# Three graph aggregations in a four-layer GNN kernel: products with the low parts of the edge counts are replaced by products with one or two copied source tiles

## The chip, the cores and the metric

The kernel runs on one core of a Trainium2 chip. The metric is the time of one execution on the device in microseconds (us), the median of several runs. Engines are named as in the profile: PE is TensorE, DVE VectorE, ACT ScalarE, POOL GpSimd, and SP the queue of the sync engine, which issues most DMAs.

## The reference

512 nodes with 512 features, 8192 edges (`src`, `dst`), four residual layers with a normalisation ahead of each. The first is a sparse attention with a feed-forward part. The second is a mean aggregation: the sum of the sources' features over a node's edges, divided by their number, through `W_l`, plus the node's own features through `W_r`, then a normalisation over the nodes. The third is two graph convolutions with self loops and degree scaling, the fourth a sum aggregation with a two-layer perceptron. What the change concerns:

```python
h = jnp.maximum(_layernorm(x), 0.0)
agg = jax.ops.segment_sum(h[src], dst, num_segments=512)      # layer 2, then divided by the degree
out = jax.ops.segment_sum(h[src] * norm[:, None], dst, n)     # layer 3, twice, with self loops
```

## The kernel before, in words

The edges are turned on the chip into a matrix of counts: how many edges go from each source node to each node. `c1` holds it by source tiles. An aggregation is then a matmul of the node features with `c1`. All matrices with 512 rows are held as four tiles of 128 rows (NT = 4).

Matmuls run in a rounded 32-bit format (`fp32r`). To keep precision, each operand is split into a high part (rounded) and a low part (the rest), and a product is made of three: high by high, high by low, low by high. For `c1` the high part is `c1_hi` (in the buffer of `q_t`) and the low part `c1_lo` (in that of `k_t`); VectorE makes them at L1009 and L1010 while the feed-forward part runs. A product of two 512 x 512 matrices has 4 x 4 matmuls of [128 x 128] by [128 x 512] per kind, so 48 in all.

TensorE runs its instructions in the order written, and waits on semaphores where it must. In the order of time:

- Attention (L1494 to L1504): 16 units `n` of two heads each. Per unit TensorE turns exponentials (`e_turn`, L1461), makes scores two units ahead (L1447) and weights values (L1476). ScalarE makes the exponentials (L507), VectorE the minima (`lowest`, L905), the weights (`weigh`, L917), every second unit a normalisation (L925 to L927), and a few side jobs tied to a unit: sums of degrees (L958, in units 5, 7, 9, 11) and an added bias (L968, in units 6, 8, 10, 12). Around the first unit ScalarE takes the four tiles of transposed counts out of PSUM (`counts_out`, L494).
- First aggregation (L1534 to L1550): for each source tile k, wait for the high part of `h1` (ScalarE, L374, `z_sb_rounded`), then 4 matmuls with the high and 4 with the low part of the counts; then 16 transposes of `h` (L1197); then 16 matmuls with the low part of `h1` (L1547; VectorE makes it at L625 in `v_sb`), the last four of which release the mean (L1030). The linear layer follows (L1562 on).
- Second aggregation (L1595, `product_by_row`, its lines L1228 and L1233): as the first, with `y` (high part by ScalarE at L512 in `v_sb`, low part by VectorE at L625 in `z_sb`). The low products go bank by bank; VectorE scales each bank (L1117) for the next layer.
- Third aggregation (L1601, `product_in_parts`, its lines L1251, L1270 and L1271): the counts are on the left; bank by bank 4 products high by high, then 4 pairs of high by low and low by high. The high part of the features comes from ScalarE (L512), the low part from VectorE (L636). Behind each bank VectorE adds, takes moments and makes layer norm coefficients (L1152 on), ScalarE makes the high part for the fourth layer (L374, `t_sb_rounded`), and that layer's aggregation with other counts (L1604) begins.

SP issues DMAs and waits in the order of its program: the blocks of the attention's edge weights (L287, from `z_sb` to `big`, ended by a wait at L292), a copy of the counts (L300), the weights (`load`, L312: `w1_0`, `w2_0`, `w_lr`, `w1_2`, `w2_2`, `w_3`, each after a matmul stage that frees its room in `big`), the four stores (L328). The load of `w1_2` (2 MB) is issued when the feed-forward part's last matmul is done, just as the first aggregation begins. The last four of the 36 rows of `big` hold no weights.

## Time and profile before

| what | us |
|---|---|
| runs: median (lowest to highest) | 397.31 (396.34 to 402.98) |
| profiled execution: span from the first to the last instruction | 395.7 |
| profiled execution: TensorE busy | 371.7 |
| profiled execution: VectorE busy, ScalarE busy | 313.2, 171.5 |

The mean granted clock of TensorE in the profiled execution is 0.992 of full speed. The profile tells of one execution by its span; what lies around the span is in the times of the runs only, whose median is 1.6 above it. Instructions of an engine can overlap, so a matmul's duration is not its share of the time. A line of the chain of waits says what the end of the kernel depended on, in order of time.

### The profile page before, as it was taken

Reading aid. Unit: us, or ns where it says so; the run is one execution under the profiler, and the core shown is the slowest. Engines: PE = TensorE matmul, PEld = TensorE weight load, DVE = VectorE, ACT = ScalarE, POOL = GpSimd, SP = SyncE. Lnnn points to the kernel's source line nnn. Section 1 sums busy time; section 2 is a strip of 40 time slices with the busy share of each in tenths; the row PEclk is TensorE's granted clock in tenths of the full one; section 3 lists DMA queues with packets and bytes.
Section 4 is the critical chain, followed back from the end, with each engine's and each line's share of the span. In section 5 each row is a group of like instructions: output and inputs, shape, how many; then the busy total and the mean of one; then the engine's idle time right before and its main releaser. Section 6 shows DMA issues by size and latency. Waiting matters only on the chain.

```text
span 395.7 us, 5097 instructions
## 1 busy us (share of the span) xinstructions
PE 371.7 (94%) x1781; PEld 282.1 (71%) x1781; DVE 313.2 (79%) x660; ACT 171.5 (43%) x287; POOL 4.2 (1%) x19
## 2 busy tenths in 40 slices
PE   2889999999988999999989999999799999999994
PEld 1555666666757888887768788887578878787873
DVE  5889999999947779997886978499875778488346
ACT  5664666444136224343467723361363531135320
POOL 4000000000000000000000000000000000000000
PEclk9999999999998999999999999999999999999998
DMA  7602444343226000056500230400420032000002
GB/s 240 247 1 69 157 154 135 104 133 110 73 85 208 2 2 1 2 188 243 206 2 1 100 114 14 198 2 0 134 81 0 2 116 96 2 0 0 2 2 104
DMA packets 16360, 32.92 MB, mean 83 GB/s; under 512 B 1360, under 2 KB 1488, under 8 KB 16336
## 3 DMA queue, kind: packets, MB, share of 16 engines
q1 hardware_dynamic: 15744, 32.25, 23.6%
q10 hardware_dynamic: 592, 0.36, 0.3%
q8 instruction: 15, 0.25, 0.3%
q14 instruction: 9, 0.07, 0.1%
HBM read 21.07 MB, written 1.05 MB: 56 GB/s over the span
## 4 chain that ended last, share of the span: by engine, by line
PE 78%; DVE 14%; ACT 4%; issue 3%; DMA 1%; DVEq 0%; ACTq 0%
PE acc L1391 11%; PE bank L1373 10%; PE bank L1476 7%; PE bank L1270 6%; PE bank L1271 6%; PE bank L1251 4%; PE acc L1251 4%; PE acc L1271 4%; PE acc L1270 4%; PE bank L1461 4%; PE acc L1447 3%; DVE big_rounded L652 2%; PE acc L1228 2%; PE bank L1228 2%; PE acc L1540 2%
## 5 line engine op out<-in xcount | busy, mean ns | idle before, releaser
L1391 PE MATMUL acc<-wide_rounded,c_rounded 128*126 128x512 f32 x200 | 58.2, 435 | 0.7 <-ACT acc L464 0.7
L1391 PEld LDWEIGHTS acc<-wide_rounded,c_rounded 128*126 128x126 f32 x200 | 37.2, 187 | 17.8 <-issue 10.7
L792 DVE TENSOR_SCALAR wide_rounded<-iota_f,picked 128x512 fp32r<-128x512 f32 x100 | 42.6, 482 | 2.1 <-issue 1.1
L483 ACT COPY z_sb<-acc 126x512 f32<-126x512 f32 x37 | 21.6, 585 | 44.9 <-PE acc L1391 36.2
L507 ACT ACTIVATE wide<-wide,low_col 128x512 f32<-128x512 f32 x32 | 21.3, 715 | 32.8 <-DVE low_col L905 32.8
L1476 PEld LDWEIGHTS bank<-v_sb,big 128*128 128x128 f32 x256 | 29.7, 192 | 4.7 <-issue 4.3
L625 DVE TENSOR_TENSOR wslot_rounded<-wslot,wide_rounded 128x512 fp32r<-128x512 f32 x24 | 16.2, 688 | 21.3 <-ACT wslot L377 21.3
L1476 PE MATMUL bank<-v_sb,big 128*128 128x65 f32 x256 | 31.6, 277 | 0.0
L798 DVE TENSOR_TENSOR c_rounded<-row_bc,wslot_rounded 128x1008 fp32r<-128x1008 bf16 x25 | 30.0, 1201 | 0.0
L1373 PE MATMUL bank<-t_sb,wslot 128*128 128x512 f32 x64 | 29.5, 594 | 0.5 <-ACT t_sb L459 0.5
L652 DVE TENSOR_TENSOR big_rounded<-big,big_rounded 128x1024 fp32r<-128x1024 f32 x24 | 29.1, 1222 | 0.4
L369 ACT ACTIVATE std<-mv,eps_c 128x1 f32<-128x1 f32 x20 | 5.8, 290 | 39.4 <-DVE mv L657 25.9
L905 DVE CUSTOM_DVE_ANT_0 wide<-acc,t_sb 128x512 f32<-128x512 f32 x32 | 20.7, 684 | 1.7 <-PE acc L1447 1.6
L917 DVE TENSOR_TENSOR big<-bank,big 128x512 f32<-128x512 f32 x32 | 20.6, 684 | 1.4 <-PE bank L1461 1.4
L1461 PE MATMUL bank<-ident,wide 128*128 128x128 f32 x128 | 18.3, 285 | 2.7 <-ACT wide L507 2.7
L1373 PEld LDWEIGHTS bank<-t_sb,wslot 128*128 128x128 f32 x64 | 12.0, 189 | 11.5 <-issue 9.6
L488 ACT COPY acc<-zero_c 126x512 f32<-126x512 f32 x33 | 19.4, 588 | 1.0
L1271 PE MATMUL acc<-big_rounded,wslot_rounded 128*128 128x512 f32 x48 | 18.7, 389 | 0.0
L1270 PE MATMUL acc<-big_rounded,wide_rounded 128*128 128x512 f32 x48 | 18.7, 389 | 0.0
L1461 PEld LDWEIGHTS bank<-ident,wide 128*128 128x128 f32 x128 | 15.0, 151 | 4.2 <-ACT wide L507 3.6
L374 ACT ACTIVATE wide_rounded<-bank,col 128x512 fp32r<-128x512 f32 x12 | 8.3, 694 | 17.4 <-PE bank L1271 17.4
L1373 PE MATMUL bank<-wslot,t_sb 128*128 128x512 f32 x32 | 15.0, 592 | 0.0
(314 smaller groups left out, 768.8 us busy)
## 6 DMA issues: line engine op xcount, KB each, us to landing
big<-z_sb SPq DMA_DIRECT2D x36, 252.0 KB
big<-in_w SPq DMA_DIRECT2D x4, 2048.0 KB, 7.8
x_sb<-in_x SPq DMA_DIRECT2D x8, 256.0 KB, 4.7
big<-in_w_3t SPq DMA_DIRECT2D x2, 1024.0 KB, 6.8
row_bc<-in_rows SPq DMA_DIRECT2D x7, 256.0 KB, 6.6
wslot<-in_wq SPq DMA_DIRECT2D x1, 1024.0 KB, 8.9
wslot<-in_wk SPq DMA_DIRECT2D x1, 1024.0 KB, 10.8
wslot<-in_wv SPq DMA_DIRECT2D x1, 1024.0 KB, 12.8
```

Source lines behind the costliest of these rows:

```text
L483: nc.scalar.copy(stage[0:BROWS, b % STAGES, :], a).then_inc(S["staged"], 1)
L507: nc.scalar.activation(e, e, ACT.Exp, bias=low_col[:, n // 4, h:h + 1], scale=-1.0).then_inc(S["e_ready"], 1)
L652: nc.vector.tensor_tensor(lo.rounded[:, part, :], lo.full[:, part, :], hi.rounded[:, part, :].bitcast(F32), ALU.subtract).then_inc(S[name ...
L792: nc.vector.tensor_scalar(hot_ring[:, u, k, :], iota_f[:, :], picked[:, 0, s0 + k:s0 + k + 1], None, ALU.is_equal)
L798: nc.vector.tensor_tensor(st_ring[:, u, :, :, :], mask[:, c, :, :].rearrange("p s a w -> p (s a) w").unsqueeze(3).broadcast_to([P, 2 * GRO ...
L1251: nc.tensor.matmul(bank[banks[m]][:, :], tile(a[0], m), r[0], start=(k == 0 and not started), stop=False)
L1270: nc.tensor.matmul(bank[b][:, :], tile(a[0], m), r[1], start=False, stop=False)
L1271: last = nc.tensor.matmul(bank[b][:, :], tile(a[1], m), r[0], start=False, stop=(k == len(terms) - 1))
L1373: ins = nc.tensor.matmul(to[:, :], left, right, start=(k == 0), stop=(k == NT - 1))
L1391: last = nc.tensor.matmul(to, st_ring[:, u, 2 * k + a, :, :].rearrange("p w k -> p (w k)"), hot_ring[:, u, k, :], start=False, stop=False, ...
L1461: last = nc.tensor.transpose(tile(bank[4 + a], t), tile(held_e[:, i % HELD, :], t), ident[:, :])
L1476: last = nc.tensor.matmul(o, by_head[:, t, h, m * P:(m + 1) * P], v_sb[:, t, h, :], start=(t == 0), stop=(t == NT - 1))
```

## The change

[...] With 8192 edges, only one source node can have more than 4096 edges to one node; with a self loop added, two can. The changed kernel multiplies with the counts' low parts of only one source tile in the first aggregation and of two in the second and third. Which tiles these are is found on the chip. ScalarE's four `counts_out` also sum the counts of each source node (`out_deg`). VectorE makes a key of each (degree times 1024 plus the node's place) in unit 3. SP copies the 512 keys into one row. VectorE takes the eight largest in unit 10, turns the first two into tile numbers and makes the second differ from the first. SP reads both numbers into registers and copies the tiles that they name (256 KB each) to fixed places, the last four rows of `big`, so that TensorE's program stays as it was built: `star_c` for the counts' low part, `star_hi` for the features' high part. TensorE waits for the copies ahead of the first product with them (`starred`, m = 0). Lines that only declare buffers and semaphores are left out below.

```diff
         bn_t = wide[:, NT:, :]
+        key_row = iota_f[0:1, :]
+        star_hi = both(lambda a: a[:, NT * KW - 4:NT * KW - 2, :], big, big_r)
+        star_c = both(lambda a: a[:, NT * KW - 2:NT * KW, :], big, big_r)
         b2_rows = [k_t_r[0:1, 0, :], k_t_r[0:1, 1, :]]
...
                              ).then_inc(S["rows_in"], 16)
+            sp.wait_ge(S["keys_ready"], 1)
+            sp.dma_start(key_row.rearrange("a (p t) -> a p t", t=NT), row_key[:, :]).then_inc(S["keys_row"], 16)
             sp.wait_ge(S["st_mm"], UNITS)
...
             load("w2_0", w2_0)
+            sp.wait_ge(S["tops_ready"], 1)
+            tops_at = [sp.value_load(top_tiles[0:1, j:j + 1], min_val=0, max_val=NT - 1) for j in range(2)]
+            def star(to, j, source, done):
+                sp.dma_start(to.rounded[:, j:j + 1, :].bitcast(F32),
+                             source.rounded[:, bass.ds(tops_at[j], 1), :].bitcast(F32)).then_inc(S[done], 16)
+            def all_hi(name):
+                hi_by, before_hi, _, _ = parts[name]
+                sp.wait_ge(S[hi_by], before_hi + NT)
             sp.wait_ge(S["ff1_mm"], FT)
...
             load("w1_2", w1_2)
+            sp.wait_ge(S["c1_parts_ready"], NT)
+            star(star_c, 0, c1_lo, "c_star_in")
+            all_hi("h1")
+            star(star_hi, 0, z_at, "h1_star_in")
             sp.wait_ge(S["lin1_mm"], NT)
             load("w2_2", w2_2)
+            sp.wait_ge(S["loops_added"], NT)
+            for j in range(2):
+                star(star_c, j, c1_lo, "loops_star_in")
+            all_hi("y")
+            for j in range(2):
+                star(star_hi, j, spare_at, "y_star_in")
             sp.wait_ge(S["gcn1_mm"], FT)
             load("w_3", w1_3t, 0)
             load("w_3", w2_3t, 1)
+            all_hi("gcn_out")
+            for j in range(2):
+                star(star_hi, j, spare_at, "gcn_star_in")
             for t in range(NT):
...
                            allow_small_or_imprecise_dtypes=True).then_inc(S["tables"], 1)
+            nc.gpsimd.iota(row_key[:, :], [[P, NT]], base=0, channel_multiplier=1,
+                           allow_small_or_imprecise_dtypes=True).then_inc(S["key_base"], 1)
             nc.gpsimd.memset(pick, 0.0).then_inc(S["pick_zeros"], 1)
...
                 act.wait_ge(S["c2_turned"], t + 1)
-                nc.scalar.copy(c1[:, t, :], bank[4 + t][:, :]).then_inc(S["c1_ready"], 1)
+                nc.scalar.activation(c1[:, t, :], bank[4 + t][:, :], ACT.Copy, accum_out=out_deg[:, t:t + 1]
+                                     ).then_inc(S["c1_ready"], 1)
             counts_out(1)
...
                     on_diagonal(rcnt_bc, rcnt_c)
+                if n == 3:
+                    dve.wait_ge(S["c1_ready"], NT)
+                    dve.wait_ge(S["key_base"], 1)
+                    nc.vector.scalar_tensor_tensor(out=row_key[:, :], in0=out_deg[:, :], scalar=float(KEYS),
+                                                   in1=row_key[:, :], op0=ALU.mult, op1=ALU.add
+                                                   ).then_inc(S["keys_ready"], 1)
+                if n == 10:
+                    dve.wait_ge(S["keys_row"], 16)
+                    link(nc.vector.max(top_keys[:, :], key_row))
+                    link(nc.vector.tensor_copy(top_i[:, :], top_keys[:, 0:2]))
+                    link(nc.vector.tensor_scalar(top_tiles[:, :], top_i[:, :], P.bit_length() - 1, NT - 1,
+                                                 ALU.logical_shift_right, ALU.bitwise_and))
+                    link(nc.vector.tensor_tensor(same_tile[:, :], top_tiles[:, 0:1], top_tiles[:, 1:2],
+                                                 ALU.is_equal))
+                    nc.vector.tensor_tensor(top_tiles[:, 1:2], top_tiles[:, 1:2], same_tile[:, :],
+                                            ALU.bitwise_xor).then_inc(S["tops_ready"], 1)
                 if n == 4:
...
                 return [((S[hi_by], before_hi + k + 1), (S[lo_by], before_lo + k + 1)) for k in range(n)]
-            def product_by_row(banks, lhs, rhs, ready, done):
+            def starred(to, m, left, right, n, done):
+                for ready in done if m == 0 else ():
+                    pe.wait_ge(S[ready], 16 * n)
+                for j in range(n):
+                    last = nc.tensor.matmul(to, tile(left.rounded[:, j, :], m), right.rounded[:, j, :], start=False,
+                                            stop=(j == n - 1))
+                return last
+            def product_by_row(banks, lhs, rhs, ready, done, star=None):
                 terms = list(zip(lhs, rhs))
                 for n, (a, r) in enumerate(terms):
                     pe.wait_ge(*ready[n][0])
-                    for i in range(2):
+                    for i in range(1 if star else 2):
                         for m, b in enumerate(banks):
...
                         last = nc.tensor.matmul(bank[b][:, :], tile(a[1], m), r[0], start=False,
-                                                stop=(n == len(terms) - 1))
+                                                stop=(not star and n == len(terms) - 1))
+                    if star:
+                        last = starred(bank[b][:, :], m, star_hi, star_c, 2, star)
                     last.then_inc(S[done], 1)
             def product_in_parts(banks, lhs, rhs, ready, done, group=1, weight_lo=None, second=None, started=False,
-                                 by_tile=0, free={}):
+                                 by_tile=0, free={}, star=None):
...
                         nc.tensor.matmul(bank[b][:, :], tile(a[0], m), r[1], start=False, stop=False)
-                        last = nc.tensor.matmul(bank[b][:, :], tile(a[1], m), r[0], start=False,
-                                                stop=(k == len(terms) - 1))
+                        if not star:
+                            last = nc.tensor.matmul(bank[b][:, :], tile(a[1], m), r[0], start=False,
+                                                    stop=(k == len(terms) - 1))
+                    if star:
+                        last = starred(bank[b][:, :], m, star_c, star_hi, 2, star)
                     last.then_inc(S[done], 1)
...
                 pe.wait_ge(*reads("h1")[k][0])
-                for i in range(2):
-                    for m in range(NT):
-                        nc.tensor.matmul(bank[m][:, :], tile(h1[k][0], m), c1s[k][i], start=(k == 0 and i == 0),
-                                         stop=False)
+                for m in range(NT):
+                    nc.tensor.matmul(bank[m][:, :], tile(h1[k][0], m), c1s[k][0], start=(k == 0), stop=False)
             pe.wait_ge(S["h_ready"], 2 * NT)
...
                 for m in range(NT):
-                    last = nc.tensor.matmul(bank[m][:, :], tile(h1[k][1], m), c1s[k][0], start=False,
-                                            stop=(k == NT - 1))
-                    if k == NT - 1:
-                        last.then_inc(S["agg1_mm"], 1)
+                    nc.tensor.matmul(bank[m][:, :], tile(h1[k][1], m), c1s[k][0], start=False, stop=False)
+            for m in range(NT):
+                starred(bank[m][:, :], m, star_hi, star_c, 1, ("c_star_in", "h1_star_in")).then_inc(S["agg1_mm"], 1)
             lo_w, hi_w = weights["w_lr"]
...
             pe.wait_ge(S["loops_added"], NT)
-            product_by_row(hi, halves(spare_at, z_at), halves(c1_hi, c1_lo), reads("y"), "agg2_mm")
+            product_by_row(hi, halves(spare_at, z_at), halves(c1_hi, c1_lo), reads("y"), "agg2_mm",
+                           star=("loops_star_in", "y_star_in"))
             product_in_parts(lo + hi, weight("w1_2", NT), halves(t_at, t_lo), reads("gcn_in"), "gcn1_mm",
...
                              weight_lo="w2_2_lo")
-            product_in_parts(hi, halves(c1_hi, c1_lo), halves(spare_at, z_at), reads("gcn_out"), "agg2b_mm")
+            product_in_parts(hi, halves(c1_hi, c1_lo), halves(spare_at, z_at), reads("gcn_out"), "agg2b_mm",
+                             star=("gcn_star_in",))
             pe.wait_ge(S["c2_ready"], NT)
```

## Rows read from the trace of the kernel before

**Rows 1.** The page: busy time of each engine, its share, instructions.

```profile
PE 371.7 (94%) x1781; PEld 282.1 (71%) x1781; DVE 313.2 (79%) x660; ACT 171.5 (43%) x287; POOL 4.2 (1%) x19
```

**Rows 2.** The chain of waits in order of time: start us, us, what.

```profile
118.03 0.59 ACT c L494
...
245.41 7.26 PE acc L1540 x32
...
288.11 7.53 PE bank L1228 x32
...
295.64 3.63 PE bank L1233 x16
...
346.62 0.91 PE bank L1251 x4
...
354.78 7.59 PE acc L1228 x32
```

**Rows 3.** The timeline of the first aggregation: start us, us, engine, line, operation.

```profile
245.44 0.37 SPq L312 DMA_DIRECT2D big<-in_w  x1
...
247.84 0.81 ACT L374 ACTIVATE z_sb_rounded<-x_sb,shift,rstd 128x512 fp32r<-128x512 f32 x1 [0.42 <-DVE shift L666]
...
252.51 1.91 PE L1197 MATMUL bank<-ident,h_sb 128*128 128x128 f32 x16
...
254.17 3.89 PE L1547 MATMUL acc<-q_t_rounded,v_sb_rounded 128*128 128x512 f32 x16
...
257.90 1.10 PE L1562 MATMUL bank<-t_sb_rounded,big_rounded 128*128 128x512 f32 x4
```

**Rows 4.** Half-microsecond window: busy us of five engines, PEclk, DMA share, GB/s.

```profile
252.00:252.50 0.50, 0.50 (x3) 0.34 (x3) 0.00 (x0) 0.00 (x0) 0.00 (x0) 1.00 0.26 98
```

**Rows 5.** The DMA issues: operands, count, KB each, median us from issue to landing.

```profile
out_x<-z_sb SPq DMA_DIRECT2D x4, 256.0 KB, 2.0
```

**Rows 6.** The timeline of SP's queue: the last copy of an attention block.

```profile
112.23 0.80 SPq L287 DMA_DIRECT2D big<-z_sb  x1
```

**Rows 7.** The waits of SP's queue: us in total, times, longest us.

```profile
SPq L292 <- DMA big<-z_sb: 2.2, 1, 2.2
```

**Rows 8.** The waits of all engines (columns as in rows 7).

```profile
PEld acc L1391 <- issue: 10.7, 41, 1.1
```

**Rows 9.** The timeline of the second aggregation.

```profile
292.01 0.82 ACT L512 ACTIVATE v_sb_rounded<-x_sb,shift,rstd 128x512 fp32r<-128x512 f32 x1
...
293.63 1.40 DVE L625 TENSOR_TENSOR z_sb_rounded<-z_sb,v_sb_rounded 128x512 fp32r<-128x512 f32 x2 [0.45 <-ACT z_sb L567]
```

**Rows 10.** The timeline of the third aggregation and the layer norm behind it.

```profile
343.54 0.69 ACT L512 ACTIVATE v_sb_rounded<-acc,dinv_c 128x512 fp32r<-128x512 f32 x1 [4.76 <-PE acc L1271]
...
344.26 0.75 DVE L636 SCALAR_TENSOR_TENSOR z_sb_rounded<-acc,dinv_c,v_sb_rounded 128x512 fp32r<-128x512 f32 x1 [4.50 <-ACT v_sb_rounded L512]
...
349.38 0.75 DVE L1152 SCALAR_TENSOR_TENSOR h_sb<-bank,dinv_c,row_bc 128x512 f32<-128x512 f32 x1 [0.30 <-PE bank L1271]
...
359.13 0.80 ACT L374 ACTIVATE t_sb_rounded<-x_sb,shift,rstd 128x512 fp32r<-128x512 f32 x1
```

**Rows 11.** One line's instructions (L422, an activation that also sums): ns min/median/max.

```profile
L422 ACT ACTIVATION_READ_ACCUMULATOR h_sb<-x_sb x2: 186/186/187, 5.7 to 6.3; 128x1 f32 x2
```

**Rows 12.** The groups by shape on VectorE: count, busy us, mean ns, idle.

```profile
L958 DVE TENSOR_REDUCE deg<-big 128x1 f32<-128x512 f32 x4 | 2.7, 676 | 0.0
...
L858 DVE TENSOR_SCALAR rounds_i<-pairs_i 1x1 int32<-1x1 int32 x1 | 0.1, 142 | 0.0
```

**Rows 13.** The timelines of ScalarE and TensorE in the attention, unit twelve.

```profile
163.88 1.33 ACT L507 ACTIVATE wide<-wide,low_col 128x512 f32<-128x512 f32 x2 [3.13 <-DVE low_col L905]
...
165.30 1.13 PE L1461 MATMUL bank<-ident,wide 128*128 128x128 f32 x8
```

**Rows 14.** Windows around two idle stretches of TensorE (columns as in rows 4).

```profile
119.50:122.50 3.00, 3.00 (x15) 3.00 (x15) 2.27 (x5) 0.75 (x2) 0.00 (x0) 0.50 1.01 290
...
282.50:284.50 2.00, 0.00 (x0) 0.00 (x0) 1.79 (x9) 0.85 (x2) 0.00 (x0) 1.00 0.78 224
```

More of the change, by code:

```diff
@@ L44 @@
 FLOOR = -3e38
+KEYS = 1024
+EXACT = 4096
+assert E < 2 * EXACT + 1 and N <= KEYS and E * KEYS + N < 2 ** 24
 ENDS, PICK, NEEDS = 130, 200, 400
@@ L134, in gnn_kernel @@
         bn_mean = sb("bn_mean", [P, NT])
+        out_deg = sb("out_deg", [P, NT])
+        row_key = sb("row_key", [P, NT])
+        top_keys = sb("top_keys", [1, 8])
+        top_i = sb("top_i", [1, 2], I32)
+        top_tiles = sb("top_tiles", [1, 2], I32)
+        same_tile = sb("same_tile", [1, 1], I32)
         rsum = sb("rsum", [P, NT, 4])
@@ L239, in gnn_kernel @@
             "agg2_mm", "agg2_ready", "gcn1_mm", "gcn1_ready", "gcn2_mm", "gcn2_ready", "agg2b_mm", "agg3_mm",
-            "agg3_ready", "gin1_mm", "gin1_ready", "gin2_mm", "b2_rows", "out_ready")}
+            "agg3_ready", "key_base", "out_degs", "keys_ready", "keys_row", "tops_ready", "c_star_in", "h1_star_in", "y_star_in",
+            "loops_star_in", "gcn_star_in", "gin1_mm", "gin1_ready", "gin2_mm", "b2_rows", "out_ready")}
         parts, made = {}, {"hi_scalar": 0, "lo_vector": 0}
```

## The prediction

> **What bounds the kernel now.** I read the busy times first: TensorE has work for 94% of the span [rows 1], so matmuls taken away should count. But its busy time is an average, so I next read the chain of waits in order of time, around the three places where the change takes matmuls away [rows 2]. The reader is to see that TensorE issues without a break in the first aggregation (32 matmuls from 245.41 in 7.26 us: 0.227 us each) and in the second (32 from 288.11, then 16 in 3.63 from 295.64). One matmul is under way for longer, but they overlap (four of them end 1.10 after the first began [rows 3]); what one gives back is the pace, and that only if the next one's operand is there. So I read the timelines of the three places for the time at which the last operand arrives, and the copies' rows for when a new one would.
>
> **The matmuls.** Each aggregation multiplies high by high, high by low and low by high parts, 16 matmuls each. The change takes out the 16 with the counts' low parts (k_t) and puts in 4, 8 and 8 with the copied tiles: 28 fewer, 6.4 us at 0.227. Their number is fixed when the program is built, whatever the counts are. All times below are on the clock of the profiled execution (span 395.7 us; the runs' median is 397.31, so 1.6 lies around the span).
>
> **First aggregation: -2.0.** TensorE now issues its first matmul at 245.24 (the chain counts it from 245.41 [rows 2]) and goes on to the linear layer at 257.90 [rows 3]. With high by high alone, the first three tiles need 12 x 0.227 = 2.7 and end at 247.96. The fourth tile's high part is written until 247.84 + 0.81 = 248.65 [rows 3], so 0.74 of the gain is a wait. From 248.70: 4 matmuls (0.91), the 16 transposes (254.17 - 252.51 = 1.66), the 16 with the low parts (257.90 - 254.17 = 3.73), 4 with the copy (0.91): 255.9 in place of 257.9, if the copy is there at 255.0. The copy of h1's tile waits for the high parts (248.7) and queues on SP behind the load of w1_2 issued at 245.44 [rows 3] and the copy of the counts' tile. The load is through by about 252.1 (in the window at 252.0 the share has fallen to 0.26) [rows 4]. Two copies of 256 KB, an eighth of the load each, are at most 2 x 6.7 / 8 = 1.7 more: 253.8, and I put 0.6 for the way to the semaphore, out of the 2.2 that a copy took in all [rows 7]: 254.4. Hidden, with 0.6 to spare; from 255.0 on each us is paid, and at 257.0 the gain is gone. VectorE's work behind (the rest of h1's transpose, weights, the mean) starts from the transposes, 2.9 earlier, so it doesn't take the 2.0 back. Bounds: -2.0 and 0.
>
> **Price of a pair of copies.** No copy from SBUF to SBUF of one [128, 512] tile stands in the trace. A store of 256 KB lands 2.0 after its issue [rows 5]; the last copy of an attention block (252 KB, SBUF to SBUF) took SP 0.80 to issue [rows 6] and 2.2 more to land [rows 7], 3.0. Both copies of a pair share a semaphore, so the second one counts: one issue later, 0.37 [rows 3] to 0.80. The source's address comes from a register, which no DMA here has; the nearest are TensorE's matmuls with such an address, which waited for their issue 41 times for 10.7 in all, 0.26 each, at most 1.1 [rows 8]. Low end 0.4 + 2.0 = 2.4, with no address work; high end 0.8 + 3.0 + 1.1 + 0.3 = 5.2; I take 2 x 0.25 + 0.4 + 2.2 = 3.1, near the store, which has the tile's form.
>
> **Second aggregation: +1.3.** The last high part of y is written until 292.83 and its low part until 295.03 [rows 9]. Before, the 16 matmuls with the counts' low parts filled the time up to 295.64. After, TensorE idles in short pieces until the fourth low part, then the wait for both copies holds it: 292.9 + 3.1 = 296.0. Two matmuls end the first bank at 296.4, and three banks of 6 (4.1) follow: 300.5 in place of 299.3. What is queued behind that wait on TensorE is all of the other banks' low products, which need no copy. Even with a copy at no cost the end is 295.1 + 21 x 0.227 = 299.9, so +0.6; at 5.2 it is +3.3. VectorE's first scaling starts at about the same time as before.
>
> **Third aggregation: +0.6.** The last high part is written until 344.23 and the low part until 345.01 [rows 10]. The pair lands at 344.3 + 3.1 = 347.4; the first bank ends at 347.8 in place of 346.6 [rows 2], d = 1.2 late, with TensorE idle for 2.0 before. The later banks take 10 matmuls, not 12 (2.3 for 2.7), but VectorE's chain of add, statistics and coefficients takes nearly 2.7 a tile itself: it idles 0.30 before the second [rows 10] and not before the others. So the last tile's high part for the next aggregation comes at 359.93 [rows 10] + d - 0.3, and TensorE, which before went through its 32 matmuls from 354.78 in 7.59 [rows 2], is through with them d - 0.6 later: +0.6. With a free copy d is -0.9 and the gain 1.5; at 5.2 it is +2.7.
>
> **Finding the tiles: +1.3.** Four copies of the counts out of PSUM also sum: a read of the accumulator of 0.186 [rows 11] and some 0.03. Two lie ahead of the first exponential, on the chain (118.03) [rows 2], one ahead of the third: +0.6; the other waits for transposes anyway. The key of 128x4 on VectorE and its copy into one row come seven units before they are needed: 0. The search is one maximum over 512 elements, priced as the reduction of 512 (0.68), and four links of 0.14 and some 0.04 between [rows 12]: 1.4. It stands ahead of unit 12's scores. Their exponentials, two from 163.88 in 1.33, end at 165.21; the first is ready at 164.55 and TensorE takes it at 165.30, the second at 165.8 [rows 13]. So 0.65 is covered: 1.4 - 0.7 = +0.7. Bounds: 0 (maximum at half that) to +1.8 (links of 0.4). SP reads the two indices after the loads of w1_0 and w2_0, while it only waits: 0. VectorE's wait for the row of keys stands ahead of all its attention work, but the row is sent seven units (some 26 us) earlier: 0, and each us that it were late would be paid in full. On SP the copies and their waits stand between the loads of w1_2, w2_2, w_3 and the stores; each waits for something that comes before the next load's own trigger, so no load moves: 0, up to the 0.6 that a copy takes of the transfer time of a load beside it.
>
> **Sum.** -2.0 + 1.3 + 0.6 + 1.3 = +1.2: 396.9 for the span, 398.5 by the runs. A measurement of this kernel tells about 2% (7.9 us) from no change; this is within it.
>
> **Rivals.** (A) The copies are cheaper than waits can see: 2.4 or less and addresses at no cost. Then -2.0, +0.6, -1.5, and +0.6 for the sums alone: -2.3, 395.0. For it: the store's 2.0 [rows 5]. Against: two issues in a row, and 3.0 for the nearest copy between SBUF tiles [rows 6, 7].
> (B) The copies sit at the high end, and the first one comes too late behind w1_2: 0 + 3.3 + 2.7 + 2.4 = +8.4, 405.7; halfway, 402. For it: SP's issue of up to 0.8 and unknown address work. Against: every copy finds an empty queue but the first.
> (C) Slower, by the clock. TensorE's granted clock is 0.50, the lower level of 1.2 GHz, through 119.5 to 122.5, behind the pause in which ScalarE empties the counts (118.03) [rows 2, 14]; yet through 282.5 to 284.5 TensorE did nothing and the clock stayed at 1.00, 2.4 GHz [rows 14]. The change makes a pause of 2.0 in the third aggregation and broken work of some 3.3 idle in 8 in the second. If either lets the clock fall for as long as at 119.5 (over 3 us busy at half pace), each costs about 1.7: 400.2 or 401.9. It passes 2% (7.9 - 1.2 = 6.7 lost) only if the low clock lasts 13.4 us of matmuls, for instance into the second graph convolution's first layer: then some 406. For: a pause of less than 2 sufficed once. Against: a longer one didn't, behind dense 512-column matmuls as here.
> The Trainium skill, in TensorE: Matmul & The Clock Gate, section "HAM oscillation — how this bites in real kernels", says that bursts of matmuls parted by waits for a DMA can find the clock gated at the start of each burst. By that rule both aggregations with a waited-for pair would start slow, and the time would be 401.9; by the row at 282.5 neither would, and it would be 398.5. The trace bears out both once, so the rule keeps a chance of its own, below the forecast's.
>
> **Chances.** Forecast (397 to 400) 0.55; A 0.16; B 0.14, a third of it past 2%; C 0.13, a quarter of it past 2%; 0.02 for a gain that I don't see. Eight in ten: from A's 395.0, a little below for the noise of the runs, to B's halfway point: 394.5 to 402.5. Slower by over 2%: 0.05 + 0.03 = 0.08, faster by over 2%: 0.02, within: 0.90.
>
> **What would show it.** Right: 1781 matmuls become 1753; the three aggregations' 48 matmuls 36, 40 and 40; from the first to the linear layer 10.7 us, not 12.7; in the second and third TensorE waits for a DMA ahead of the first copied product, some 0.7 and 2.0; from the copied y's last high part to its landing 3.1; in unit 12 TensorE waits 0.7 for ScalarE. Wrong: no such wait (A), waits of 3 and more (B), a granted clock under 1.00 behind 296 or 347 (C), or SP late for the first copy, so that the linear layer waits.

## The result, and the profile after

The changed kernel takes 400.46 us (median of 20 runs, 398.05 to 404.4), the kernel before, beside it, 398.52 (20 runs, 396.34 to 403.14): a ratio of 1.0056, 95% interval 1.003 to 1.0082. By the ratio that is 2.2 us more, between 1.2 and 3.3. The ratio leaves out each kernel's slowest runs, so it is not quite that of the two medians, which are 1.9 apart. I had forecast +1.2 us and no change by a measurement of 2%.

The matmuls went as the program says:

```profile
PE 373.4 (93%) x1753; PEld 279.8 (70%) x1753; DVE 314.4 (78%) x666; ACT 172.1 (43%) x291; POOL 4.2 (1%) x20
```

28 fewer than in [rows 1], and yet TensorE is busy for 373.4 us and not 371.7. (That the low parts left out are zero is the program's own premise: it takes counts of up to 4096 for exact, `EXACT` in the kernel. The runs give times and say nothing on it.) The reason for the longer busy time is the granted clock: the profiled execution (403.44 us, span 401.7) is one of the long ones, and TensorE stood at 0.50, the lower level of 1.2 GHz, in four pieces of some 3.4 us; e1 below, with the same 1753 matmuls and two such pieces, is busy for 368.2. In a window (busy us of TensorE, PEclk, DMA share, GB/s) one of them looks so:

```profile
350.00:352.00 2.00, 2.00 (x6) 0.50 0.00 0
```

In the profile of before there is one such piece under work (119 to 123 us, [rows 14]) and one behind the last matmul. A busy share, and a whole span, therefore can't be compared between two single executions here. What can be is the length of a stretch between two events, where the clock stood at full speed in both. I cut the kernel at first matmuls and read the same six stretches from the timelines of every kernel. A star marks a stretch in which the clock fell while TensorE still had work.

| from ... to (us) | before | after | e1 | e2 | e3 | e4 | e5 | e6 | e7 | e8 | e9 |
|---|---|---|---|---|---|---|---|---|---|---|---|
| first scores ... first turned exponentials | 4.82 | 6.45* | 4.99 | 4.82 | 4.99 | 5.00 | 4.81 | 7.10* | 6.47* | 4.99 | 5.00 |
| unit 11 ... unit 12 of the attention | 3.70 | 4.94 | 3.70 | 3.71 | 4.94 | 4.94 | 3.70 | 3.70 | 4.94 | 4.94 | 4.94 |
| first aggregation ... first keep-warm matmul | 40.02 | 38.05 | 37.88 | 38.05 | 38.34* | 37.90 | 38.08 | 38.01 | 37.92 | 38.00 | 38.34* |
| keep-warm ... first matmul behind the second aggregation | 13.85 | 15.48 | 15.47* | 15.43 | 14.57* | 15.47* | 13.82 | 13.85 | 15.04* | 15.47 | 15.20* |
| from there ... first matmul behind the product with the second counts | 66.82 | 69.01* | 67.47 | 67.46 | 66.83 | 65.66 | 66.80 | 65.69 | 67.53 | 67.50 | 67.54 |
| from there ... end | 29.77 | 31.16* | 31.08* | 31.17* | 29.45 | 31.14* | 29.53 | 31.13* | 31.07* | 31.21* | 29.55 |

**First aggregation.** The timeline of after (start us, us, engine, line, operation; in brackets the idle time ahead and what ended it), against [rows 3]:

```profile
248.00 2.89 PE L1613 MATMUL acc<-q_t_rounded,z_sb_rounded 128*128 128x512 f32 x12
251.46 1.20 PE L1613 MATMUL acc<-q_t_rounded,z_sb_rounded 128*128 128x512 f32 x4 [0.57 <-ACT z_sb_rounded L417]
...
254.15 3.92 PE L1619 MATMUL acc<-q_t_rounded,v_sb_rounded 128*128 128x512 f32 x16
258.02 1.16 PE L1285 MATMUL acc<-big_rounded 128*128 128x512 f32 x4
259.02 1.08 PE L1633 MATMUL bank<-t_sb_rounded,big_rounded 128*128 128x512 f32 x4
```

From the first matmul to the linear layer it takes 11.0 us, 12.66 before; the wait for the fourth tile's high part is there (0.57), and the profile marks no wait for the copies. The queue's timeline and the median from issue to landing say when they came:

```profile
248.69 0.57 SPq L336 DMA_DIRECT2D big_rounded<-k_t_rounded  x1
251.54 0.52 SPq L336 DMA_DIRECT2D big_rounded<-z_sb_rounded  x1
```

```profile
big_rounded<-v_sb_rounded SPq DMA_DIRECT2D x4, 256.0 KB, 2.4
...
big_rounded<-z_sb_rounded SPq DMA_DIRECT2D x1, 256.0 KB, 6.4
```

251.54 + 6.4 = 257.9: behind the load of w1_2 the copy landed just when it was wanted, where an empty queue brings one in 2.4. A narrower window of TensorE's timeline shows the last three matmuls ahead of the first copied product:

```profile
257.23 0.84 PE L1619 MATMUL acc<-q_t_rounded,v_sb_rounded 128*128 128x512 f32 x3
```

From there to that product, at 258.02, are 0.79 us, where three matmuls at 0.227 take 0.68. So TensorE was held by 0.1, too little to be marked as a wait. In e4, where the copy landed at 265.07 and the product began at 265.24, the same stretch is 0.68.

**Second and third aggregation.** Rows of the chain of waits, in order of time:

```profile
294.32 2.37 DMA big_rounded<-v_sb_rounded
296.82 0.70 PE bank L1285 x2
...
347.18 2.42 DMA big_rounded<-v_sb_rounded
349.64 1.16 PE bank L1285 x2
```

A DMA now stands on the path twice, where [rows 2] had matmuls. ScalarE's timeline has the last high parts that are copied:

```profile
292.80 0.81 ACT L556 ACTIVATE v_sb_rounded<-x_sb,shift,rstd 128x512 fp32r<-128x512 f32 x1
...
345.93 0.69 ACT L556 ACTIVATE v_sb_rounded<-acc,dinv_c 128x512 fp32r<-128x512 f32 x1 [4.75 <-PE acc L1343]
```

In the second, y's last high part was ready at 293.61, the second copy landed at 296.69 and TensorE went on at 296.82, 3.2 later; in the third the times are 346.62, 349.60 and 349.64, 3.0. TensorE waited 0.44 and 1.55 for them, where I had put some 0.7 and 2.0.

**Unit 12 of the attention.** The search stands on VectorE (MAX8 and four links) ahead of the rest of what it does for this unit. After:

```profile
163.95 0.67 DVE L1017 MAX8 top_keys<-iota_f 1x8 f32<-1x512 f32 x1
...
165.22 0.15 DVE L1023 TENSOR_TENSOR top_tiles<-top_tiles,same_tile 1x1 int32<-1x1 int32 x1
...
165.29 0.67 DVE L1028 TENSOR_TENSOR h_sb<-h_sb,row_bc 128x512 f32<-128x512 f32 x1
...
166.61 1.33 ACT L551 ACTIVATE wide<-wide,low_col 128x512 f32<-128x512 f32 x2 [4.47 <-DVE low_col L949]
...
167.12 1.27 DVE L961 TENSOR_TENSOR big<-bank,big 128x512 f32<-128x512 f32 x2
...
167.94 1.23 PE L1535 MATMUL bank<-ident,wide 128*128 128x128 f32 x8 [1.08 <-ACT wide L551]
```

The search took 1.34 us (163.95 to 165.29; priced 1.4), and TensorE's turning of the exponentials waited 1.08.

### The profile page after: what moved, and what is told of

Same layout as the page of the kernel before. It is cut to its first block, busy times and chain, and to the rows that moved or that the text cites. A ratio compares the mean times of both kernels' runs of the same rounds, so it can differ in the third digit from the quotient of the medians.

```text
span 401.7 us, 5075 instructions
## 1 busy us (share of the span) xinstructions
PE 373.4 (93%) x1753; PEld 279.8 (70%) x1753; DVE 314.4 (78%) x666; ACT 172.1 (43%) x291; POOL 4.2 (1%) x20
## 4 chain that ended last, share of the span: by engine, by line
PE 75%; DVE 13%; ACT 6%; issue 2%; DMA 2%; SPq 0%; DVEq 0%; ACTq 0%
PE acc L1465 11%; PE bank L1447 10%; PE bank L1550 6%; PE bank L1341 5%; PE bank L1343 5%; PE acc L1322 4%; PE bank L1322 4%; PE acc L1341 4%; PE acc L1343 4%; PE bank L1535 3%; PE acc L1521 3%; DVE stats L700 1%; PE bank L1637 1%; PE bank L1633 1%; PE bank L1638 1%
## 5 line engine op out<-in xcount | busy, mean ns | idle before, releaser
L1465 PEld LDWEIGHTS acc<-wide_rounded,c_rounded 128*126 128x126 f32 x200 | 37.2, 187 | 17.8 <-issue 10.7
L1447 PE MATMUL bank<-t_sb,wslot 128*128 128x512 f32 x64 | 29.5, 594 | 0.5 <-ACT t_sb L502 0.5
## 6 DMA issues: line engine op xcount, KB each, us to landing
wslot<-in_wk SPq DMA_DIRECT2D x1, 1024.0 KB, 10.7
```

Of the source, the lines that this page charges most:

```text
L1447: ins = nc.tensor.matmul(to[:, :], left, right, start=(k == 0), stop=(k == NT - 1))
L1465: last = nc.tensor.matmul(to, st_ring[:, u, 2 * k + a, :, :].rearrange("p w k -> p (w k)"), hot_ring[:, u, k, :], start=False, stop=False, ...
```

## The experiments

My theory behind the result: the first aggregation gains its 2.0 us, and finding the tiles, the waits of the second and those of the third give back more. The rival: the stages are as good as equal, and what separates the kernels is where the clock falls. Each kernel was timed against the kernel before; the intervals are some 0.35% (1.4 us) to each side, so single terms are read from the table above and the runs only bound their sum.

**e1: without the search.**

```diff
+            nc.gpsimd.iota(top_tiles[:, :], [[1, 2]], base=0, channel_multiplier=0).then_inc(S["tops_ready"], 1)
...
-                    link(nc.vector.max(top_keys[:, :], key_row))
...
```

> Leaves out the search: the five instructions on VectorE that find the two tiles (MAX8, copy, shift, compare, xor) are gone and the copies take tiles 0 and 1, written as constants at the start; accumulator reads, key row and its DMA stay. Stage read: from TensorE's first bias matmul behind the pair loop (112.44 in before, 112.26 in the changed kernel) to the first matmul of the first aggregation (245.24 and 248.00), 132.8 us before and 135.7 us changed. My theory (the search delays VectorE and with it the attention by its full 1.35 us, not by the 0.7 that I forecast): 134.4 us, and the run's time 1.35 us below the changed kernel's (some 399.1, +0.15% over before). Rival (the search lies in VectorE's slack, and the growth at unit 12 is another thing's): 135.7 us, time as the changed kernel (400.5, +0.5%).

Measured: 398.89 us, ratio 0.999 (0.9959 to 1.0021), below the changed kernel's interval. Unit 11 to 12 is back at 3.70 us. The stage as defined there is 131.75 us and not 134.4, since two of the four falls of the clock in the profile of after lay in it, and none did here; e3, with the search and likewise no fall, has 133.12. So the search costs 1.37 us of the attention, nothing of it hidden: 1.24 at unit 12 and 0.1 from there to unit 13 (3.88 in e3, 3.78 here). The timelines say why:

```profile
163.12 1.28 DVE L962 TENSOR_TENSOR big<-bank,big 128x512 f32<-128x512 f32 x2
...
164.05 1.12 PE L1528 MATMUL bank<-ident,wide 128*128 128x128 f32 x8
```

The turning writes a bank that VectorE must have emptied of the unit before (`p_ready`). The two instructions shown overlap; one takes 0.68 (the page's mean). So the first ends at 163.12 + 0.68 = 163.80, and TensorE starts at 164.05. In after the same instruction ends at 167.12 + 0.68 = 167.80, and TensorE starts 0.14 behind it; so the cover here was 164.05 - 163.94 = 0.1 us. The profile puts the wait down to ScalarE, whose first exponential had been done since some 167.3.

**e2: the finding moved out of the attention.**

```diff
-                nc.scalar.activation(c1[:, t, :], bank[4 + t][:, :], ACT.Copy, accum_out=out_deg[:, t:t + 1]
+                nc.scalar.copy(c1[:, t, :], bank[4 + t][:, :]).then_inc(S["c1_ready"], 1)
...
+            for t in range(NT):
+                mark(nc.vector.tensor_reduce(out_deg[:, t:t + 1], c1[:, t, :], AX.X, ALU.add))
...
+                if t == 0:
+                    dve.wait_ge(S["keys_row"], 16)
```

> Nothing left out; the whole finding is moved out of the attention: counts_out copies without an accumulator, VectorE sums the rows of the counts with four reductions (0.68 us each) in its 4.96 us of waiting in the first feed-forward, the keys' DMA goes then, and the search stands in VectorE's 1.66 us wait of the first row tile of the layer norm ahead of the first aggregation. Theory (finding costs the attention 1.35 us for the search and 0.6 to 1.4 for the accumulator reads ahead of the exponentials): the same stage falls from 135.7 to 132.8..133.8 us and the run by 2.0 to 2.8 us to 397.7..398.5, at or below the kernel before. Rival (the attention's loss is the clock's, not the finding's): the stage stays at 135 or more, the time above 399.5. A second rival (the work moved comes onto the path there): the stretch of the layer norm ahead of the first aggregation is 1.3 us longer and the time as in the run without the search.

Measured: 398.52 us, ratio 1.0001 (0.9962 to 1.0039); the stage 132.2 us, a little below what I expected (one fall of the clock lay in it, two in the profile of after), unit 11 to 12 3.71 us. The new places cover all of it: VectorE's timeline

```profile
205.85 2.46 DVE L1039 TENSOR_REDUCE out_deg<-c 128x1 f32<-128x512 f32 x4
...
210.89 0.69 DVE L668 TENSOR_TENSOR wslot_rounded<-wslot,wide_rounded 128x512 fp32r<-128x512 f32 x1 [2.39 <-ACT wslot L420]
...
232.09 0.68 DVE L1070 MAX8 top_keys<-big 1x8 f32<-1x512 f32 x1
...
233.84 0.69 DVE L668 TENSOR_TENSOR v_sb_rounded<-h_sb,z_sb_rounded 128x512 fp32r<-128x512 f32 x1 [0.32 <-ACT h_sb L420]
```

still shows 2.39 and 0.32 us of waiting behind what was put in. Both rivals fall. The accumulator reads are seen at the first turned exponentials: 4.82 us without, 4.99 to 5.00 with them. ScalarE's timelines, e1 (with the sums) and then before:

```profile
117.37 0.60 ACT L538 ACTIVATE c<-bank 128x512 f32<-128x512 f32 x1 [3.74 <-PE bank L1552]
117.86 0.20 ACT L538 ACTIVATION_READ_ACCUMULATOR c<-bank 128x1 f32 x1
117.95 0.59 ACT L538 ACTIVATE c<-bank 128x512 f32<-128x512 f32 x1
118.43 0.20 ACT L538 ACTIVATION_READ_ACCUMULATOR c<-bank 128x1 f32 x1
118.52 1.33 ACT L552 ACTIVATE wide<-wide,low_col 128x512 f32<-128x512 f32 x2
```

```profile
117.55 1.07 ACT L494 COPY c<-bank 128x512 f32<-128x512 f32 x2 [3.74 <-PE bank L1485]
118.51 1.35 ACT L507 ACTIVATE wide<-wide,low_col 128x512 f32<-128x512 f32 x2
```

Two copies with their reads hold ScalarE for 1.15 us, two plain ones for 0.96: the read begins 0.11 before the activation ends and the next starts 0.11 before the read ends, so a read of 0.20 costs 0.09.

**e3: only the first aggregation changed.**

```diff
-            for j in range(2):
-                star(star_c, j, c1_lo, "loops_star_in")
...
-            product_by_row(hi, halves(spare_at, z_at), halves(c1_hi, c1_lo), reads("y"), "agg2_mm",
-                           star=("loops_star_in", "y_star_in"))
+            product_by_row(hi, halves(spare_at, z_at), halves(c1_hi, c1_lo), reads("y"), "agg2_mm")
...
-            product_in_parts(hi, halves(c1_hi, c1_lo), halves(spare_at, z_at), reads("gcn_out"), "agg2b_mm",
-                             star=("gcn_star_in",))
+            product_in_parts(hi, halves(c1_hi, c1_lo), halves(spare_at, z_at), reads("gcn_out"), "agg2b_mm")
```

> The second and third aggregations multiply all their low parts again, as before; the first stays changed, and so does the finding of the tiles. Theory (the copies' waits cost the second 1.6 us and the third 0.6 at full clock): the second stage (first keep-warm matmul ahead of the second aggregation to the first matmul of the product behind it) is back to its 14.3 us, the third (first matmul of the third aggregation to the end of the product with the second counts) to 22.6 us, TensorE waits for no DMA in either, and the time falls by about 2.2 us to 398.3 (0 to +0.1% over before). Rival (these stages cost nothing in the undisturbed runs, only the clock makes them look so): the time stays at 400.5.

Measured: 398.98 us, ratio 1.0014 (0.9984 to 1.0044). The third stretch is back at 66.83 us. The second is 14.57, with a fall of the clock ahead of the aggregation; in e5 and e6, where it is also as before, it is 13.82 and 13.85. The kernels with a changed second aggregation have 15.43 to 15.48, whether the clock fell ahead of it or not: there TensorE waits anyway. (e7 has another order; in e9 the fall straddles the cut, and its 38.34 and 15.20 add up to 53.54, as after's 38.05 and 15.48 to 53.53.) So the second costs 1.6 us and the third 0.65, at full clock, and the rival falls.

**e4: the third aggregation's moving operand by register.**

```diff
-            all_hi("gcn_out")
-            for j in range(2):
-                star(star_hi, j, spare_at, "gcn_star_in")
...
+                    if right is spare_at:
+                        moving = right.rounded.rearrange("p k n -> p (k n)")[:, bass.ds(tops_at[j] * N, N)]
...
```

> Nothing left out; in the third aggregation the starred products read their moving operand straight from the high part by an address in a register of TensorE (its two loads stand ahead of the first aggregation), their weights are the copies that the second aggregation already had; the two late copies and the wait for them are gone. Theory (the third pays for the wait, 1.55 us, and has 8 matmuls of some 0.23 us less than before): the third stage is 22.6 - 1.8 = 20.8 us at full clock, the run 2.4 us or more below the changed kernel (398.0), and the clock doesn't fall in it. Rival 1 (a matmul by register is dear): above 0.3 us more for each of its eight, the stage back at 22.6 or more, no gain. Rival 2 (what runs behind the stage, not TensorE, bounds it): the wait goes and the stage's end stays within 0.5 us.

Measured: 399.36 us, ratio 1.0002 (0.9965 to 1.004). The third stretch is 65.66 us, 1.16 below before and 1.8 below the changed kernel at full clock (67.47 in e1 and e2), as the theory has it; both rivals fall. The run's interval is too wide to add to that. The products by register cost what the others do (0.62 for two that overlap, as with the copies):

```profile
355.11 0.62 PE L1285 MATMUL bank<-v_sb_rounded,big_rounded 128*128 x2
```

Of the 1.8 us of matmuls less, 0.6 are lost to the layer norm behind (below, e9). The profiled execution, 407.28 us, shows what a long fall of the clock costs: behind the search's wait the clock stayed low for 20 us. TensorE's timeline, and windows of five engines with PEclk, DMA share and GB/s:

```profile
166.62 1.63 PE L1535 MATMUL bank<-ident,wide 128*128 128x128 f32 x8 [1.07 <-ACT wide L548]
```

```profile
160.00:164.00 4.00, 4.00 (x34) 3.42 (x35) 3.17 (x13) 0.81 (x2) 0.00 (x0) 1.00 0.02 4
...
168.00:172.00 4.00, 4.00 (x19) 3.08 (x17) 2.08 (x6) 1.34 (x2) 0.00 (x0) 0.50 0.00 0
...
184.00:188.00 4.00, 4.00 (x22) 4.00 (x22) 2.38 (x6) 0.00 (x0) 0.00 (x0) 0.53 0.10 35
```

From unit 12's first turned exponentials to unit 15's it took 18.5 us in it and 10.9 in after. In the six profiles with the search in the attention the clock fell behind this wait in two (e4, and e8 for 10 us); in the five without that wait never. So few profiles don't show that the wait is the cause.

**e5: the first aggregation alone, with the finding late.** The edits of e2 and e3 together.

> Only the first aggregation starred, and the finding moved out of the attention as in e2. Theory: what is left is the gain of the first aggregation, 2.0 us (38.0 us from its first matmul to the first keep-warm matmul, against 40.0 before), nothing given back: ratio 0.995, some 397.1 where before has 399.1. Rival (that gain is taken up later in the kernel, as by the wait for the y parts ahead of the second aggregation): that stretch shortens and the next, to the first matmul behind the second aggregation, is longer than its 13.85 us by as much; ratio 0.998 to 1.002.

Measured: 397.91 us, ratio 0.9953 (0.9915 to 0.9991), as the theory has it; the next stretch is 13.82 us, so nothing is taken back.

**e6: with the third by register too.** The edits of e2 and e4 together, and the second aggregation as before.

> The same with the third aggregation starred too, its moving operand read by register and its weights the two copies of the counts' low parts fetched after the loops are added; the second multiplies all low parts as before. Theory: 2.0 us from the first and 1.16 from the third (65.66 us in e4 against 66.82 from the first matmul behind the second aggregation to the first behind the third product): 3.2 us, ratio 0.992, faster than both kernels. Rival (the clock falls behind a shortened third aggregation: in all four profiles with a starred third it fell some 13 us behind it, in none of the two without): the last stretch is 31.1 us instead of 29.6, ratio 0.995 to 0.997.

Measured: 395.9 us, ratio 0.9931 (0.9896 to 0.9965): below the kernel before by more than the interval, though well within the 2%, and, by intervals that are apart, below the changed one. The stretches give -1.97 and -1.13, -0.78%, inside the interval. In its third aggregation TensorE goes on without a wait:

```profile
345.41 1.09 PE L1338 MATMUL bank<-z_sb_rounded,q_t_rounded 128*128 128x512 f32 x4
346.34 0.62 PE L1282 MATMUL bank<-v_sb_rounded,big_rounded 128*128 x2
```

The last stretch was 31.13 us, with a fall of the clock in it, as the rival said of the profile; the run's ratio lies between the two expectations.

**e7: the second's copied products at the end.**

```diff
-                    if star:
-                        last = starred(bank[b][:, :], m, star_hi, star_c, 2, star)
-                    last.then_inc(S[done], 1)
+                    if not star:
+                        last.then_inc(S[done], 1)
+                for m, b in enumerate(banks if star else ()):
+                    starred(bank[b][:, :], m, star_hi, star_c, 2, star).then_inc(S[done], 1)
```

> The changed kernel with one order changed: the second aggregation multiplies the low parts of all four row tiles first and the starred tiles at the end. Theory (the second stage pays 0.44 us for the copies and about 1.2 because the removed matmuls had filled the time in which the high parts come one by one): TensorE no longer waits for a DMA there, the stretch from the first keep-warm matmul to the first matmul behind the second aggregation falls from 15.45 to 14.9 us (0.4 to 0.8 less), still 1 us over before. Rival (all of the 1.6 us is the copies'): it falls to 13.9 us. Rival 2 (row tile 0, now finished 2.7 us later, bounds the product behind it): 15.4 us or more. Run time 400.

Measured: 400.07 us, ratio 1.0016 (0.9976 to 1.0056); the stretch 15.04 us, between the theory's 14.9 and rival 2.

```profile
293.27 1.21 PE L1297 MATMUL bank<-q_t_rounded,v_sb_rounded 128*128 128x512 f32 x4 [0.41 <-ACT v_sb_rounded L556]
...
295.48 3.23 PE L1302 MATMUL bank<-q_t_rounded,z_sb_rounded 128*128 128x512 f32 x13 [0.20 <-DVE z_sb_rounded L669]
298.55 1.98 PE L1285 MATMUL bank<-big_rounded 128*128 128x512 f32 x8
300.70 1.63 PE L1331 MATMUL acc<-t_sb_rounded,big_rounded 128*128 128x512 f32 x6 [0.18 <-ACT t_sb_rounded L556]
```

No DMA is waited for, 0.2 us of the next product's wait for row tile 0 come in, and still the stretch is 1.2 us over before. Of the 1.6 the copies' lateness is some 0.4; the rest fits the last parts of y (argued, not shown by a run of its own): in after TensorE waits for four of them, 0.37, 0.43, 0.41 and 0.20 us, and it waited for none before, when the matmuls taken out ran in that time.

**e8: filler matmuls in the third's wait.**

```diff
+                    if star and m == 0:
+                        keep_warm(lo[0], 6)
```

> The changed kernel with six filler matmuls (those of the keep-warm function, into a free bank) in TensorE's wait for the copies of the third aggregation. They change no result and cost nothing while the wait of 1.55 us lasts. Theory (the wait itself costs its 0.6 us against before, whatever the clock does; a fall of the clock in it is an accident of some executions): the stretch from the first matmul behind the second aggregation to the first behind the third product stays at 67.4 to 67.5 us, as in e1 and e2 at full clock, and the time at some 400.4. Rival (the pause makes the clock fall in most executions, at 1.5 us each): the median falls by 1 us or more against the changed kernel's, and no low clock follows the third aggregation.

Measured: 400.57 us, ratio 1.0038 (0.9999 to 1.0076); the stretch 67.50 us.

```profile
350.14 1.47 PE L1354 MATMUL acc<-ident_b 128*128 128x512 bf16 x6
351.85 0.73 PE L1285 MATMUL bank<-big_rounded 128*128 128x512 f32 x2 [0.23 <-DMA big_rounded<-v_sb_rounded]
```

The pause is filled but for 0.23, the copies come no sooner, and the time is the changed kernel's as far as the intervals tell. The rival falls: in the four profiles with the unfilled wait (after, e1, e2, e7) the clock fell in it once.

**e9: the third's first row tile finished later.**

```diff
+                    if star and m == 0:
+                        continue
+                    for i in (0, 1) if star and m == 1 else (m,) if star else ():
...
```

> The changed kernel with one order changed: in the third aggregation the starred products of the first row tile stand behind the second row tile's eight full products (some 1.85 us), so that the copies land before TensorE comes to them; copies and instructions are the same. Theory (the third stage's +0.64 us against before is the wait of 1.55 less 8 matmuls and what waits for the high parts behind it): no wait for a DMA there, the stretch from the first matmul behind the second aggregation to the first behind the third product falls from 67.46 us at full clock to 65.7, as by register in e4, and the run by some 1.8 us against the changed kernel's. Rival (the first row tile, finished 2.3 us later, makes the product behind it wait by as much): 67 us or more, the time unchanged.

Measured: 399.32 us, ratio 1.0018 (0.9983 to 1.0053), the stretch 67.54 us. Here my theory fell by the stretch, and the rival held: TensorE waits for no DMA in it, and pays the same at the next product. (The run alone wouldn't decide: its ratio is 1.5 us below the changed kernel's, by intervals that overlap.) The timeline:

```profile
348.19 1.09 PE L1285 MATMUL bank<-big_rounded 128*128 128x512 f32 x4
...
348.85 0.75 DVE L1212 SCALAR_TENSOR_TENSOR h_sb<-bank,dinv_c,row_bc 128x512 f32<-128x512 f32 x1 [3.04 <-PE bank L1285]
...
353.87 0.81 ACT L417 ACTIVATE t_sb_rounded<-x_sb,shift,rstd 128x512 fp32r<-128x512 f32 x1 [2.25 <-DVE shift L710]
...
354.82 2.11 PE L1297 MATMUL acc<-wslot_rounded,t_sb_rounded 128*128 128x512 f32 x8 [0.93 <-ACT t_sb_rounded L417]
```

VectorE's layer norm takes 2.3 to 2.6 us a row tile from the first one on and can't start before that one is finished. It starts at 348.85 here, 4.7 behind the stage's first matmul (344.14), and as late in e1, with the wait; in e4 it is 2.9, before 3.3. VectorE's timelines of before (first matmul at 343.34) and e1 (341.56):

```profile
346.66 0.75 DVE L1152 SCALAR_TENSOR_TENSOR h_sb<-bank,dinv_c,row_bc 128x512 f32<-128x512 f32 x1 [1.65 <-PE bank L1271]
```

```profile
346.25 0.75 DVE L1205 SCALAR_TENSOR_TENSOR h_sb<-bank,dinv_c,row_bc 128x512 f32<-128x512 f32 x1 [3.02 <-PE bank L1278]
```

This chain, not TensorE, sets when the next product goes on.

## Why the prediction was right, and where it wasn't

The verdict and the range held, and so did the account: the four terms at full clock, from the table, are

- **First aggregation: -2.0 forecast, -1.97 measured** (40.02 to 38.05). That the two agree so closely is partly luck: the whole 2.0 was to come up to the linear layer (10.7 us forecast), where 1.64 came (11.02), and the other 0.33 came behind it, where I had put nothing; why stays open. The copy was hidden but for 0.1 us, by a margin of nothing and not of 0.6. The step that failed is the landing at 254.4. The load of w1_2 is issued 2.75 later in after, so that is 257.15 there, and the copy landed at 257.9. The way to the semaphore took the 0.6 that I put; the two copies added more transfer time than the 1.7 that I called the most. Windows of after (columns as in [rows 4]):

```profile
257.00:257.50 0.50, 0.50 (x4) 0.42 (x3) 0.50 (x1) 0.00 (x0) 0.00 (x0) 1.00 0.49 184
257.50:258.00 0.50, 0.50 (x3) 0.15 (x2) 0.50 (x1) 0.00 (x0) 0.00 (x0) 1.00 0.00 0
```

The transfers end about 257.25, 9.1 behind the load's issue at 248.19, where I had read 6.7 for the load alone: 2.4 for the two.

- **Price of a pair: 3.1 forecast, 3.1 and 3.0 measured** from the last high part to the landing (3.2 and 3.0 to TensorE's start): 0.7 and 0.6 to the second issue, and 2.4 from there. An address in a register cost no more than that. Rivals A and B fall with it.
- **Second aggregation: +1.3 forecast, +1.62 measured.** The mechanism was as described. The term was mis-sized in its last step: from the end of the wait to the next product I had 4.5 us (20 matmuls at 0.227), and it took 4.7; and before's next product began at 299.11, not 299.3. With a copy at no cost I had +0.6; e7 gives 1.2 with the copy out of the way, by another order, 0.2 of it a wait of its own.
- **Third aggregation: +0.6 forecast, +0.65 measured** (66.82 to 67.47). That the layer norm's chain, and not TensorE's wait, carries the lateness on, e9 showed by taking the wait away for nothing. Two small errors cancel in the number: the first bank came 1.4 late, not 1.2, and the chain behind it took 2.3 to 2.6 us a tile, not nearly 2.7.
- **Finding the tiles: +1.3 forecast, +1.55 measured**, and here two steps failed against each other. The search was to have 0.65 of cover, since TensorE takes the exponentials at 165.30 that are ready at 164.55 [rows 13]. It had 0.1: TensorE also waits for VectorE to empty the bank, and that instruction was late by the whole search. The row was there to be read in before:

```profile
164.37 1.28 DVE L917 TENSOR_TENSOR big<-bank,big 128x512 f32<-128x512 f32 x2
```

Its first instruction ends at 165.05, 0.25 ahead of TensorE's start; with the 0.14 that TensorE starts behind it, 0.1 is left. So 1.37 for 0.7. The accumulator reads I counted at 0.186 and 0.03 for each of three: they are overlapped at both ends, 0.09 each, and only two are on the path: 0.18 for 0.6.

The sum is -1.97 + 1.62 + 0.65 + 1.55 = +1.85 us for my +1.2, and the runs say +2.2 (1.2 to 3.3). The same sums for the other kernels (e1 +0.5, e2 +0.3, e3 -0.4, e4 0.0, e5 -2.0, e6 -3.1, e7 +1.4, e8 +1.9, e9 +1.9) all lie within their runs' intervals, and but for e7's 15.04 the stretches that they come from have no star: the rival, that only the clock separates the kernels, falls. The forecast of 398.5 us stood on 397.31, a median of 3; with 20 runs before has 398.52, and the same sum would have said 399.7.

**Rival C** came about in part: the clock fell behind the third's wait in the profile of after (69.01 us for 67.47: 1.5, priced 1.7), but in one of four such waits, and in none of the six profiles behind the second's. The Trainium skill, in TensorE: Matmul & The Clock Gate, section "HAM oscillation — how this bites in real kernels", tells of a kernel whose every burst behind a DMA wait starts at the low clock; the waits there last some 3 to 5 us. I had stretched that to any wait for a DMA; here the waits were 0.44 and 1.55 us, and a start at the low clock behind them was the exception. Where the clock bit hardest was a place that I hadn't named, the wait in unit 12.

What stays open: how much of the changed kernel's median is falls of the clock. The runs without a profile give their time and the mean granted clock, but not where it fell. The median clock is 0.985 in the changed kernel's 20 runs, and 0.986 to 0.987 in the 87 runs of before beside e1 to e9, hardly more; and the shortest runs of after and before, 398.05 and 396.34, lie 1.7 apart, near the sum of 1.85. Both speak against a large share. But the last stretch shows how uncertain it is: it had a fall (31.1 us, not 29.5) in seven of the eight profiles with a changed third aggregation and in none of the three without; but e9, one of the eight, is free of it. e6's runs (-0.69%) lie nearer to its sum without such a fall (-0.78%) than with one in each run (-0.4%), which their interval doesn't exclude.

## What to carry to other kernels

Matmuls taken off a busy TensorE pay only where their operands were already there: the first aggregation gave 2.0 of the 2.7 us that its twelve would have taken, the second less than nothing, because the matmuls removed had filled the arrival of the others' operands. If what replaces them needs data that is copied after the last operand is ready, some 3 us of copying stands on the path; read from place (here the moving operand, by register) it cost nothing that these runs show. And before an instruction is put on an engine "with slack", look at every semaphore of its next consumer, since the profile names one releaser and the one behind it may be as late.

## What I had not expected of the hardware

- A pause of 1.07 us in the attention was followed by 20 us (e4) and 10 us (e8) at half clock, at a price of 7.6 us in e4 between units 12 and 15 alone (18.5 for 10.9), and in four other profiles the same pause by none. Pieces of some 3.4 us were the rule elsewhere (e6 had one of 13.7 at the attention's start).
- A copy of 256 KB between SBUF tiles took 2.3 to 2.4 us from issue to landing in an empty queue (one pair in e7 2.8 and 3.6); behind a load of 2 MB it landed 0.2 to 1.3 us after the load did, 6.2 to 9.6 from its own issue, in every profile.
- A matmul whose moving operand has its address in a register ran at the pace of the others, where the pair loop's matmuls with register addresses had waited 0.26 us each for their issue [rows 8].
